# Gated cross-attention layer: four steps' scores in one piece in five groups of the first half

## What is computed

```
q = rope(layernorm(x) @ wq)          # 32 heads of 128
k = rope(ctx @ wk); v = ctx @ wv     # 8 key/value heads, each for 4 query heads
attn = softmax(q k^T / sqrt(128) + mask) @ v
x = x + tanh(g_xattn) * (attn @ wo)
e = argmax(layernorm(x) @ route_w^T)          # one of 8 experts per token
x = x + tanh(g_ffn) * weight * (B_e (A_e layernorm(x)))
```

## Time and profile before

| | us |
|---|---|
| median of 3 runs | 1053.43 (1052.4 to 1053.97) |
| profiled execution | 1053.14 |
| its span, first to last instruction | 1051.3 |
| PE busy | 1041.6 (99%) |
| DVE busy | 873.7 (83%) |
| ACT busy | 634.8 (60%) |
| POOL busy | 592.2 (56%) |
| DMA queue q1, share of 16 engines | 57.1% |

### The profile page before, as it was taken

One profiled execution on the slowest core, in us unless ns is written; L12 is line 12 of the kernel. 1 busy time (PEld: TensorE's weight loads), 2 busy tenths in 40 slices (PEclk: granted clock), 3 DMA queues, 4 the chain that ended last, 5 costly groups with the idle time before them and its releaser, 6 DMA issues.

```text
span 1051.3 us, 19132 instructions
## 1 busy us (share of the span) xinstructions
PE 1041.6 (99%) x6663; PEld 864.9 (82%) x6663; DVE 873.7 (83%) x1423; ACT 634.8 (60%) x1112; POOL 592.2 (56%) x518
## 2 busy tenths in 40 slices
PE   9999999999999999999999999999999999999998
PEld 7888888877788888888888888888888888888786
DVE  7875766788888888888888899888887878787997
ACT  6564466676767666767666645556564655555653
POOL 4552379887878787878764433334343434444423
PEclk9999999999999999999999999999999999999999
DMA  7768966576765656565569844564454545443102
GB/s 263 266 224 299 396 235 245 159 264 219 250 212 180 225 182 216 186 198 206 162 225 397 270 148 154 171 201 145 156 176 134 181 146 169 163 147 131 47 25 81
DMA packets 106094, 206.40 MB, mean 196 GB/s; under 512 B 8848, under 2 KB 58640, under 8 KB 100112
## 3 DMA queue, kind: packets, MB, share of 16 engines
q1 hardware_dynamic: 105424, 204.40, 57.1%
q10 hardware_dynamic: 576, 0.79, 0.2%
HBM read 122.31 MB, written 82.84 MB: 195 GB/s over the span
## 4 chain that ended last, share of the span: by engine, by line
PE 88%; DVE 5%; POOL 2%; issue 1%; DMA 1%; SPq 1%; ACT 1%; DVEq 0%; POOLq 0%
PE attn L998 31%; PE proj L925 26%; PE attn L867 7%; PE turned L867 4%; PE score L867 4%; PE score L947 3%; PE attn L983 3%; PE attn L985 3%; PE turned L958 3%; PE small L947 2%; PE proj L842 1%; DVE acc L1353 1%; PE proj L947 1%; POOL rot L1958 1%; DVE stats L1206 1%
## 5 line engine op out<-in xcount | busy, mean ns | idle before, releaser
L998 PE MATMUL attn<-wo_s,o_s 128*128 128x512 f32 x1524 | 375.1, 395 | 0.6 <-DVE o_s L1341 0.5
L925 PE MATMUL proj<-xB,wq_s 128*128 128x512 f32 x1344 | 334.2, 391 | 0.0
L998 PEld LDWEIGHTS attn<-wo_s,o_s 128*128 128x128 f32 x1524 | 280.7, 188 | 58.6 <-DVE o_s L1341 1.5
L925 PEld LDWEIGHTS proj<-xB,wq_s 128*128 128x128 f32 x1344 | 251.4, 188 | 51.4 <-issue 0.4
L1958 POOL TENSOR_TENSOR rot<-rot,tab 128x512 f32<-128x512 f32 x110 | 163.2, 1484 | 146.9 <-ACT rot L1677 146.7
L1241 DVE TENSOR_TENSOR q_r<-q_r,tab 128x512 f32<-128x512 f32 x127 | 114.5, 902 | 1.5 <-ACT x_third L1677 1.4
L1341 DVE TENSOR_TENSOR o_s<-attn,o_s 128x512 fp32r<-128x512 f32 x127 | 82.4, 685 | 32.0 <-ACT o_s L1726 32.0
L1698 ACT ACTIVATE copies<-proj 128x512 f32<-128x512 f32 x96 | 57.5, 599 | 80.7 <-PE proj L925 80.5
L1726 ACT ACTIVATE o_s<-attn 128x512 fp32r<-128x512 f32 x127 | 69.2, 596 | 56.7 <-PE attn L985 56.6
L1353 DVE SCALAR_TENSOR_TENSOR acc<-attn,gates_t,acc 128x512 f32<-128x512 f32 x127 | 94.9, 748 | 10.2 <-PE attn L998 7.8
L1958 POOL TENSOR_TENSOR rot_third<-rot_third,tab 128x512 f32<-128x512 f32 x40 | 61.7, 1542 | 57.5 <-ACT rot_third L1677 54.7
(11 more groups left out here) (277 smaller groups left out, 1735.8 us busy)
## 6 DMA issues: line engine op xcount, KB each, us to landing
wq_kept<-wq_s SPq DMA_DIRECT2D x16, 1792.0 KB, 6.5
wq_s<-wq_kept SPq DMA_DIRECT2D x16, 1792.0 KB, 7.8
v_kept<-vst SPq DMA_DIRECT2D x64, 256.0 KB, 4.3
v_s<-v_kept SPq DMA_DIRECT2D x128, 128.0 KB, 5.0
wo_kept<-wo_s SPq DMA_DIRECT2D x32, 512.0 KB, 6.4
wo_s<-wo_kept SPq DMA_DIRECT2D x32, 512.0 KB, 5.4
k_kept<-kst SPq DMA_DIRECT2D x32, 256.0 KB, 2.1
wq_raw<-in_wq SPq DMA_DIRECT2D x16, 512.0 KB, 7.7
```

The source lines that it names most:

```text
L925: last = e.matmul(dst[:, :], wq_s[:, b % 2, A, s, kt, :], xB[:, B, mv, kt, :], start=(first and kt == 0 and m == 0), stop=(kt == 1 and m = ...
L998: last = e.matmul(out_bank(k, bp)[:, :], o_s[:, s, bp, h, :], wo_s[n % WO_SLOTS][:, m, :], start=(h == 0 and i == 0), stop=(h == GROUP - 1 ...
```

## The change

`QUADS` gets the groups 2 to 6 as well (steps 8 to 27). Two places are written for these groups alone (condition `in_quad(k) and k < HALF_STEPS`): in step two DVE makes both `prob_low` ahead of `q_add`, and in step three PE makes product 0 ahead of `times_values(k - 1)`, and ACT copies it ahead of `attn_high`. POOL's code for `combine_weights` in step one is the same again as in other groups; it had been written otherwise for quads that have no such work, so nothing of it changes in either half.

```diff
-QUADS = range(9, 15)
+QUADS = (*range(2, 7), *range(9, 15))
...
-                for b, i in first[:1] if quad_begins(k) else ():
+                ahead = quad_begins(k) or k % 4 == 2 and in_quad(k) and k < HALF_STEPS
+                for b, i in first[:1] if ahead else ():
                     product(b, i)
                 times_values(k - 1)
...
+                lows_first = k % 4 == 1 and in_quad(k) and k < HALF_STEPS
+                if lows_first:
+                    prob_low(k, 0, 1)
+                    for q in ropes[0]:
+                        q_add(*q)
+                    add_out(k - 1, 1)
...
-                if quad_begins(k) and pieces:
-                    combine_weights(pieces[0][0])
                 subtract_max(k)
...
-                    if not quad_begins(k):
-                        combine_weights(pieces[0][0], (0,))
+                    combine_weights(pieces[0][0], (0,))
```

More of the change, by code:

```diff
@@ L1113, in _ @@
                 between(k, 1)
-                for b, i in first[:1] if not quad_begins(k) else ():
+                for b, i in first[:1] if not ahead else ():
                     product(b, i)
@@ L1517, in _ @@
                 together = k % 4 == 3 or (k, 6) in EXTRA
+                lows_first = k % 4 == 1 and in_quad(k) and k < HALF_STEPS
[4 more added lines that the diff above has]
+                    add_out(k - 1, 1)
+                    between(k, 7)
+                    between(k, 8)
+                    expert_norms_begin(norms_of(k))
+                    continue
                 if quad_begins(k):
@@ L1792, in _ @@
                 between(k, 0)
-                for p in first if quad_begins(k) else ():
+                ahead = quad_begins(k) or k % 4 == 2 and in_quad(k) and k < HALF_STEPS
+                for p in first if ahead else ():
                     copy_product(*p)
@@ L1800, in _ @@
                 between(k, 1)
-                for p in first if not quad_begins(k) else ():
+                for p in first if not ahead else ():
                     copy_product(*p)
@@ L2031, in _ @@
                     combine_weights(HEAD_PAIRS + 1, (1,))
-                if k % 2 == 0 and pieces and not quad_begins(k):
+                if k % 2 == 0 and pieces:
                     combine_weights(pieces[0][0], (1,) if k > 2 else (0, 1))
```

## The result

The changed kernel takes 1064.66 us (1064.47 to 1065.25, 4 runs) against 1053.63 in the runs of the kernel before beside it: ratio 1.0108, 95% interval 1.0096 to 1.012. The profiled execution took 1065.25 with a span of 1063.5, 12.2 us more than before's 1051.3.

What follows compares the result with a forecast made beforehand. PE, busy 1041.6 of 1051.3 us, was taken to bound the kernel. Gain -1.65, step-four waits +8.5 and group starts +2.2 gave +9.1 us: 1062.5 us, in a range of 1055.5 to 1066.5.

Steps and rivals of the forecast that it cites:

- Gain of one piece: PE's list in groups 2 to 6: fewer changes between fp32 and fp32r matmuls save 0.33 us each, 1.65 in all.
- Wait ahead of step four's times_values: PE waits in step four for low halves and the freed bank: 1.82 us in each of groups 2 to 5.
- L1334 and L1354: Sign in the new profile: PE's step-four waits name p_low and acc, once per group, together 1.5 to 2 us.
- Group 6: Steps three and four split no weights there, so PE's wait ahead of step four's times_values is 1.23 us.
- Start of a group: Third piece of scores waits for rope j = 3, delayed by POOL's raw_low: 0.44 us in five groups, 2.2 in all.
- the upper bound of the group's start: 0.9 us a group if add_out ahead of the first times_values and step one's probabilities are late as well.
- rival 3: The lag carries on into rope, low halves and add_out at the group's start: +12.2 us, 1065.6; chance 0.15.
- Moved at no cost: Keys are fetched a step sooner into a free slot, and step four's last product ahead of project_out waits for nothing.
- the first (helpers keep up): DVE and POOL keep up in groups 2 to 6, only the gain stays: 1051.8 us, 0.16% faster; chance 0.12.
- The second: POOL and DVE block each other less, chain 8.26 us, group starts cost nothing: +3.7 us, 1057.1; chance 0.14.
- The fourth: One piece of scores gains nothing on PE, as by the page on TensorE: 1064.2 us; chance 0.03.

Runs made afterwards that it cites:

- light kernels: Changed kernel and kernel before, each with POOL writing only 8 columns of most wq and wo low halves: 1052.27 us and 1051.72 us.
- the first experiment: Changed kernel without its two helper edits (DVE's prob_low order in step two, PE's product 0 in step three): 1063.49 us, ratio 1.0096.
- `v4`: `v2` with POOL's two weight_low around step four's subtract_max one place later each, in groups 2 to 5: 1059.81 us, ratio 1.0063.
- `light_quads`: Changed kernel with POOL's weight_low and raw_low writing only 8 columns in the first half's steps, computation incomplete: 1052.27 us, ratio 0.9991 to the kernel before.
- `xb_first`: Changed kernel with the three last blocks of x fetched ahead of the 1.8 MB of wq in step 28: 1063.15 us, ratio 1.0092.
- `group6`: Kernel before with only group 6 made in one piece, with its two helper edits: 1055.65 us, ratio 1.0019.
- `v2`: `v1` with add_out(k - 1, 1) ahead of q_add in step three: 1058.74 us, ratio 1.0048.
- `v1`: Changed kernel with both raw_low moved, low halves ahead of q_add, POOL's step-three wait for q_add dropped, blocks of x first: 1059.96 us, ratio 1.0062.
- `no_edits`: Changed kernel without its two helper edits, in steps two and three: 1063.49 us, ratio 1.0096.
- `acc_first`: Changed kernel with DVE's both prob_low and add_out(k - 1, 1) ahead of q_add in step three, groups 2 to 6: 1071.56 us, ratio 1.0172.
- `pool_late`: Changed kernel with POOL's raw_low of wo moved from step two's end to step three behind by_sin, groups 2 to 6: 1066.05 us, ratio 1.0124.

## Why the prediction was right, and where its sizes were off

The call (slower, 1062.5 in a range of 1055.5 to 1066.5) held, by the mechanism it named. By its own steps:

- **Gain of one piece**: predicted 0.33 a group, from two groups of different halves. Without waits it is 0.22 (light kernels, 51.00 to 50.78). The two halves differ in more than their scores. The gain is small but not the 0 that follows from the page "TensorE: Matmul & The Clock Gate" of the Trainium skill (section "Back-to-back issue gap"): 1.2 us in five groups.
- **Wait ahead of step four's times_values**: freed bank predicted at 25.68 us after step two's, PE's second part at 25.73; it came at 25.65. Against PE's own 23.74 that is 1.91 a group, predicted 1.82. The exponential did come sooner (row sum 1.74 us after subtract_max's start instead of 2.05), but subtract_max itself came later (15.01 instead of 14.78), so that of the 0.34 us I had half of, 0.08 were there. The 8.85 us from row sum to freed bank stood to the hundredth (DVE's list there is the same, eleven instructions to the low halves and not twelve). Both edits shift the wait and don't remove it, as said, and as the first experiment shows. The profile puts these waits down to "issue", not to L1334 and L1354 as expected; that they are meant follows from the 0.11 and 0.05 us between their ends and PE's starts.
- **Group 6**: predicted 1.23 and 0.44 less the gain; the group costs 1.31 alone and 1.40 over its light form.
- **Start of a group**: raw_low did make the third piece late, but one operation sooner than I had it. by_sin holds the q_cos of j = 2 (1.19 us), raw_low (363.71 to 365.45) the q_add of j = 2 (1.60 us), and j = 3 follows at its own length. The third piece alone is 0.25 late and 0.35 with what hangs on it, predicted 0.44. That q_add is held by POOL is in line with the page "SBUF — State Buffer" of the Trainium skill (section "SBUF: two separate sides"); `v4`'s 1.81 us is the plainest row for it.
- **Small change**: none was counted in the forecast; the upper bound of the group's start and rival 3 named some. Put beside `light_quads` place by place, PE's list in group 2 is longer by 0.40 us at the third piece of scores, 0.07 at the turned probabilities of step one, 0.17 at those of step four, 1.73 at step four's times_values and 0.19 at the second part of the next step one's, which waits for add_out. Some of this is not the wait itself: behind a wait the next matmul comes 0.07 to 0.11 us later than in the list without waits. Together groups 2 to 5 cost 2.49 each over their light form (53.27 - 50.78), against 1.82 + 0.44 = 2.26 predicted. Over the five groups: 11.4 of waits less 1.2 of gain, 10.2 against 9.1.
- **Moved at no cost** is the step that failed. I looked at keys and at their slot, and at nothing else on SP's list. But taking two pieces of scores out of step 26 shortens the stretch in which a full queue must reload 7 MB: 1.5 us in step 29. That the order of the transfers decides is shown by `xb_first`, that group 6 alone brings it by `group6`. In the trace of before the same two products took 3.05 us instead of 2.90, which was a sign of it. It needed the view of transfers for steps 24 to 29, where the queue is as full (102.1% from 541 to 577 us).

These add to 10.25 + 1.5, and 0.34 more stand before step 6, where nothing differs. The profiled execution was also the slowest of the four, 0.6 over their median.

So the call was no luck, but the number owes something to the width of the range: the forecast was 2.2 us short, of which 1.5 are a term that it didn't have. The measured time is nearer to rival 3's 1065.6 than to the forecast. Yet rival 3's terms are not what happened: step four's wait was 1.91 and not 1.99, and the start of a group cost some 0.6, between the forecast's 0.44 and rival 3's 0.9.

Of the rivals, the first (helpers keep up) is what `light_quads` does, and only with 10 us less of POOL's work a group. Its case that an ordering might do it was tested by `v2`: the wait it speaks of can be ordered away, but other waits and pauses of 0.6 to 2.2 us a group (over the light form's 50.78) take its place. The second, that an ordering makes it cost only part, is where `v2` without its pauses would stand. The fourth, no gain from one piece, was a third right: 0.11 of the 0.33 us weren't there.

## To carry to other kernels

Work that a busy engine does between two hand-overs is also time given to its helpers. Moving 2.2 us of it to another place, even where it runs a little better, takes these 2.2 us from every chain that ends in between, and from transfers in a full queue too; so look up what is due in the stretch that gets shorter, transfers included, before the stretch that gets longer. If POOL and DVE are at 80% with operations that hold each other up, an order that helps one hand-over costs another: cutting their work took 12 us off the changed kernel, the best of the orders tried 6.

## What was not expected of the hardware

- A DVE operation with two SBUF inputs that meets one of POOL ends some 0.54 us after POOL's end, over and over: 1.60 instead of 0.69 us beside by_sin, raw_low and weight_low, 1.81 where POOL's began 0.02 us sooner.
- A wait of PE costs somewhat more than its length: the next matmul came 0.07 to 0.11 us later than in the same list without waits (group 2 beside `light_quads`).
- PE can pause for 0.2 to 1.4 us inside a run of short like matmuls with no semaphore there: eleven times in seven kernels, always at one of the same three places of its list, and always until 2.2 to 2.6 us after a packet of the instruction queue began. It happened with waits in the group before (`no_edits`, `acc_first`) and not at all in `light_quads`, which has none. Why the packets come later in some kernels is open.
- A long wait of PE can cost twice: in `pool_late` the granted clock fell to its lower level after 2.92 us without a matmul, and the next twelve matmuls took 1.6 us more. In the other kernels PE's waits in these steps, up to 1.5 us, left it full.
- The view of waits names no releaser for most transfers that are late: they stand as "issue", as do the waits ahead of times_values where low halves and bank come close together. In `v1`, where the bank alone was late, it names `acc`.
